# LayerNorm of an attention result: from node blocks on partitions to features on partitions

## What is computed

```python
def _layernorm(x, axis=-1, eps=1e-05):
    m = jnp.mean(x, axis=axis, keepdims=True)
    v = jnp.var(x, axis=axis, keepdims=True)
    return (x - m) / jnp.sqrt(v + eps)

# layer 0, attention over the edges, H = 4 heads of C = 32 features
ex = jnp.exp(alpha - amax[dst])
denom = jax.ops.segment_sum(ex, dst, num_segments=N)
alpha = ex / (denom[dst] + 1e-16)
msg = xj * alpha[..., None]
out = jax.ops.segment_sum(msg, dst, num_segments=N)

x = _layernorm(x + attention(x))        # the change is in this line
x = _layernorm(x + message_passing(x))  # three rounds of message passing
```

## Time and profile before

| | |
|---|---|
| Time, median of 3 runs | 10751.08 us (10739.96 to 10765.35) |
| The profiled execution, its own time | 10651.89 us |
| Span of the profiled execution | 10649.8 us |
| Busy share of the span | PE 45%, PEld 39%, DVE 47%, ACT 14%, POOL 56% |
| Mean granted TensorE clock | 0.511 of full speed |

### The profile page before, as it was taken

One profiled execution on the slowest core, in us unless ns is written; L12 is line 12 of the kernel. 1 busy time (PEld: TensorE's weight loads), 2 busy tenths in 40 slices (PEclk: granted clock), 3 DMA queues, 4 the chain that ended last, 5 costly groups with the idle time before them and its releaser, 6 DMA issues.

```text
span 10649.8 us, 148443 instructions
## 1 busy us (share of the span) xinstructions
PE 4842.9 (45%) x27078; PEld 4162.2 (39%) x27079; DVE 4985.9 (47%) x26801; ACT 1465.7 (14%) x5798; POOL 5973.7 (56%) x6332
## 2 busy tenths in 40 slices
PE   4555555555564444444445444444445444444445
PEld 3444444444453333333334333333334333333334
DVE  5545555545565444444445444444444444444445
ACT  2222222222232000000002000000002000000002
POOL 3444444444444666666663666666663666666664
PEclk6555555555555555555556555555555555555555
DMA  4333333333323333333333333333333333333333
GB/s 109 86 86 87 87 85 86 86 87 85 85 71 119 108 108 108 108 108 108 108 108 104 108 108 108 108 108 108 108 108 103 108 108 108 108 107 108 108 108 84
DMA packets 755854, 1076.13 MB, mean 101 GB/s; under 512 B 325952, under 2 KB 554464, under 8 KB 755268
## 3 DMA queue, kind: packets, MB, share of 16 engines
q0 software_dynamic: 301056, 822.48, 27.0%
q1 hardware_dynamic: 448148, 247.94, 8.7%
q10 hardware_dynamic: 6356, 3.20, 0.1%
HBM read 1027.54 MB, written 45.47 MB: 101 GB/s over the span
## 4 chain that ended last, share of the span: by engine, by line
another core or an unknown queue 45%; DVE 24%; issue 18%; PE 8%; DVEq 3%; DMA 0%; ACT 0%; SPq 0%; POOL 0%; ACTq 0%; POOLq 0%
DVE junk L1389 8%; PE ps L1588 3%; DVE ps L1368 2%; DVE pen L1378 2%; DVE acc L1409 2%; DVE selw L1398 2%; DVE junk L1026 1%; PE ps L1673 1%; PE ps L1577 1%; PE ps L1683 1%; PE ps L1585 1%; DVEq L1368 1%; PE ps L1659 1%; DVEq L988 1%
## 5 line engine op out<-in xcount | busy, mean ns | idle before, releaser
L603 POOL DMA_INDIRECT G<-mp_rows,idx x4704 | 4446.0, 945 | 2914.6 <-issue 1379.4
L1683 PE MATMUL ps<-selw,G 128*128 128x32 f32 x9408 | 2223.6, 401 | 989.2 <-issue 427.5
L1378 DVE TENSOR_TENSOR pen<-ps,G 128x512 f32<-128x512 f32 x1176 | 808.3, 687 | 3923.4 <-remote 3635.6
L1683 PEld LDWEIGHTS ps<-selw,G 128*128 128x128 f32 x9408 | 2094.2, 328 | 1272.5 <-issue 1215.9
L603 POOL DMA_INDIRECT G<-gat_rows,idx x1568 | 1487.9, 949 | 1551.2 <-ACT idx L682 1074.8
L1673 PE MATMUL ps<-awin,ring 96*128 96x128 bf16 x4704 | 717.2, 308 | 3155.0 <-DVE ring L1363 2989.1
L1673 PEld LDWEIGHTS ps<-awin,ring 96*128 96x128 bf16 x4704 | 486.6, 147 | 3260.9 <-DVE ring L1363 3081.5
L816 ACT ACTIVATE gate<-logit,cur 128x4 f32<-128x4 f32 x1176 | 349.6, 297 | 6503.1 <-issue 4053.1
L1389 DVE SCALAR_TENSOR_TENSOR junk<-pen,ps 128x128 f32<-128x128 f32 x4704 | 1061.2, 279 | 0.1
L1577 PE MATMUL ps<-sel,ex 128*4 128x32 f32 x3136 | 231.0, 238 | 1381.2 <-DVE tt L1150 1357.5
L1363 DVE TENSOR_TENSOR ring<-ring,ps 96x512 bf16<-96x512 bf16 x1176 | 796.4, 677 | 0.4
(11 more groups left out here) (182 smaller groups left out, 5409.3 us busy)
## 6 DMA issues: line engine op xcount, KB each, us to landing
ring<-rel_dst SPq DMA_DIRECT2D x1176, 96.0 KB
G<-mp_rows,idx POOLq DMA_INDIRECT x4704
ring<-rel_dst SPq DMA_DIRECT2D x392, 128.0 KB
awin<-mp_dst_rows SPq DMA_DIRECT2D x1176, 24.0 KB
G<-gat_rows,idx POOLq DMA_INDIRECT x1568
mp_rows<-acc SPq DMA_DIRECT2D x30, 640.0 KB, 3.3
mp_dst_rows<-acc SPq DMA_DIRECT2D x30, 480.0 KB
gat_rows<-ring SPq DMA_DIRECT2D x50, 128.0 KB, 2.0
```

Source lines behind the costliest of these rows:

```text
L603: pool.indirect_dma_start(out=G[:, u, width * t:width * (t + 1)], out_offset=None, in_=table, in_offset=bass.IndirectOffsetOnAxis(ap=idx[: ...
L1378: v.tensor_tensor(pen[:, off % 2, :].rearrange("p (t c) -> p t c", t=T), PS[off % 2][:, :].rearrange("p (t c) -> p t c", t=T), Grows[:, of ...
L1683: i = mm(PS[2 + off % 2][:, 0:W], Grows[:, off % U, t, 0:D], selw[:, off % 4, W * t:W * t + W], start=(t == 0), stop=(t == T - 1))
```

## The change

Nothing is turned. Chunks of 512 nodes (`LNC = 512`; `NLN = 13`, the last one 256 wide) are worked on as they lie, features on the partitions. POOL adds 1e-16 to the whole of the denominators; DVE takes the reciprocal of the whole 128x512 and multiplies; POOL adds `xT`, which is there already. The mean is taken off by a matmul with the matrix `centre` (identity minus 1/128): its product is y minus the mean over the features, on every partition. ACT squares it from PSUM, a matmul with a matrix of 1/128 gives the variance on every partition, ACT takes the root, DVE takes the reciprocal of 128x512 and multiplies into `hT`, and ACT copies `hT` to `xT`. The second load of x falls away, `weighted` is half as large, and two constants are made at the start (`centre`, `mean`) instead of one (`dsel`).

`ln_steps` writes out the order with lags, as `node_steps` does: on DVE, in one step, the second reciprocal of chunk s-3, the first reciprocal of chunk s, the scaling of chunk s-3, the product of chunk s.

```diff
+    LNC = 512
+    NLN = -(-NP // LNC)
...
+        def ln_steps(order):
+            for step in range(NLN + max(lag for lag, stage in order)):
+                for lag, stage in order:
+                    if 0 <= step - lag < NLN:
+                        stage(step - lag)
...
-            sp.wait_ge(gat["acc"], NG)
-            for b in range(NBLK):
-                load_x(b // BL, b % BL)
...
-            node_steps(pool, NT // 2, ((5, ln_residual),), BL)
+            def ln_safe_den(c):
+                nc.gpsimd.tensor_single_scalar(acc[:, 1, ln_nodes(c)], acc[:, 1, ln_nodes(c)], 1e-16,
+                                               ALU.add).then_inc(ln_safe, 1)
+            def ln_residual(c):
+                pool.wait_ge(ln_gat, c + 1)
+                nc.gpsimd.tensor_tensor(acc[:, 0, ln_nodes(c)], acc[:, 0, ln_nodes(c)], xT[:, ln_nodes(c)],
+                                        ALU.add).then_inc(ln_y, 1)
+            pool.wait_ge(gat["acc"], NG)
+            ln_steps(((1, ln_residual), (0, ln_safe_den)))
...
-            node_steps(act, NT // 2, ((0, ln_block), (7, ln_sqrt), (10, ln_to_x1), (10, ln_to_h)), BL)
+            def ln_square(c):
+                act.wait_ge(ln_yc, c + 1)
+                nc.scalar.activation(acc[:, 1, ln_nodes(c)], PS[c % 3][:, 0:ln_width(c)], ACT.Square).then_inc(ln_sq, 1)
+            def ln_sqrt(c):
+                act.wait_ge(ln_var, c + 1)
+                nc.scalar.activation(acc[:, 1, ln_nodes(c)], PS[3 + c % 3][:, 0:ln_width(c)], ACT.Sqrt,
+                                     bias=epsc[:, 0:1]).then_inc(ln_sd, 1)
+            def ln_to_x1(c):
+                act.wait_ge(ln_h, c + 1)
+                nc.scalar.copy(xT[:, ln_nodes(c)], hT[:, ln_nodes(c)]).then_inc(ln_x1, 1)
+            ln_steps(((1, ln_square), (2, ln_sqrt), (4, ln_to_x1)))
...
-            then(v.tensor_scalar(dsel[:, :], iotaF[:, 0:H], float(C), pF[:, 0:1], ALU.mult, ALU.is_equal))
+            then(v.tensor_single_scalar(centre[:, :], ident[:, :], 1.0 / D, ALU.subtract))
+            then(v.memset(mean[:, :], 1.0 / D))
...
-            node_steps(dve, NT // 2, ((8, ln_deviation), (6, ln_stats), (9, ln_scale), (2, ln_dens), (7, ln_mean_var),
-                                      (3, ln_recip), (4, ln_divide)), BL)
+            def ln_divide(c):
+                dve.wait_ge(ln_safe, c + 1)
+                v.reciprocal(acc[:, 1, ln_nodes(c)], acc[:, 1, ln_nodes(c)]).then_inc(ln_rden, 1)
+            def ln_weigh(c):
+                dve.wait_ge(ln_rden, c + 1)
+                v.tensor_tensor(acc[:, 0, ln_nodes(c)], acc[:, 0, ln_nodes(c)], acc[:, 1, ln_nodes(c)],
+                                ALU.mult).then_inc(ln_gat, 1)
+            def ln_recip(c):
+                dve.wait_ge(ln_sd, c + 1)
+                v.reciprocal(acc[:, 1, ln_nodes(c)], acc[:, 1, ln_nodes(c)]).then_inc(ln_rs, 1)
+            def ln_scale(c):
+                dve.wait_ge(ln_rs, c + 1)
+                v.tensor_tensor(hT[:, ln_nodes(c)], PS[c % 3][:, 0:ln_width(c)], acc[:, 1, ln_nodes(c)],
+                                ALU.mult).then_inc(ln_h, 1)
+            ln_steps(((3, ln_recip), (0, ln_divide), (3, ln_scale), (0, ln_weigh)))
...
-            node_steps(pe, NT // 2, ((9, ln_back), (1, ln_turn)), BL)
+            def ln_centre(c):
+                if c >= 3:
+                    pe.wait_ge(ln_h, c - 2)
+                pe.wait_ge(ln_y, c + 1)
+                mm(PS[c % 3][:, 0:ln_width(c)], centre[:, :], acc[:, 0, ln_nodes(c)], start=True, stop=True).then_inc(ln_yc, 1)
+            def ln_variance(c):
+                if c >= 3:
+                    pe.wait_ge(ln_sd, c - 2)
+                pe.wait_ge(ln_sq, c + 1)
+                mm(PS[3 + c % 3][:, 0:ln_width(c)], mean[:, :], acc[:, 1, ln_nodes(c)], start=True, stop=True).then_inc(ln_var, 1)
+            ln_steps(((2, ln_variance), (1, ln_centre)))
```

More of the change, by code:

```diff
@@ L43 @@
 PREP_IDENT = 10
-PREP_CONST = PREP_IDENT + 11
+PREP_CONST = PREP_IDENT + 12
 PREP_REL = PREP_CONST + 5
@@ L181, in gnn_kernel @@
         junk = sb("junk", [P, GE])
-        weighted = sb("weighted", [P, 4, T * D])
-        R = weighted[:, 0:2, :]
+        weighted = sb("weighted", [P, 2, T * D])
+        R = weighted[:, :, :]
         ex4 = sb("ex4", [P, 2, T * H])
@@ L244, in gnn_kernel @@
         fbcol = sb("fbcol", [P, 1])
-        dsel = sb("dsel", [P, H])
+        centre = sb("centre", [P, D])
+        mean = sb("mean", [P, D])
         WT = sb("WT", [P, D])
@@ L335, in gnn_kernel @@
         ln_y = sem("ln_y")
-        ln_st = sem("ln_st")
-        ln_mv = sem("ln_mv")
+        ln_yc = sem("ln_yc")
+        ln_sq = sem("ln_sq")
+        ln_var = sem("ln_var")
         ln_sd = sem("ln_sd")
         ln_rs = sem("ln_rs")
-        ln_rows = sem("ln_rows")
-        ln_x1T = sem("ln_x1T")
         ln_x1 = sem("ln_x1")
@@ L379, in nodes, with ln_nodes, ln_width @@
             return bass.ds(turn * (per * NB) + off * NB, NB)
+        def ln_nodes(c):
+            return slice(c * LNC, min(c * LNC + LNC, NP))
+        def ln_width(c):
+            return min(LNC, NP - c * LNC)
+        def ln_steps(order):
[3 more added lines that the diff above has]
+                        stage(step - lag)
         def spare(off):
@@ L1234, in _ @@
                 dve.sem_inc(x_free, 1)
[L1237 to L1284, removed]
-                if reached(n, off, BU):
-                    dve.wait_ge(ln_x1T, n + (off - BU + 1))
-                v.tensor_scalar(x1rows[0:NB, u, :], grows[0:NB, u, :], bmv[0:NB, u, 0:1], brs[0:NB, u, :],
-                                ALU.subtract, ALU.mult).then_inc(ln_rows, 1)
@@ new lines, in ln_recip @@
+            def ln_recip(c):
[6 more added lines that the diff above has]
+            ln_steps(((3, ln_recip), (0, ln_divide), (3, ln_scale), (0, ln_weigh)))
+            dve.wait_ge(ln_x1, NLN)
@@ L1294, in _ @@
+            dve.wait_ge(ln_h, NLN)
             dve.sem_inc(l_bn, 1)
```

33 lines of the change are left out of this document (1 added, 32 removed).

## The result

The changed kernel takes 10796.69 us (median of 8 runs, 10789.73 to 10804.40), the kernel before in the same comparison 10755.14 us (median of 8, 10739.96 to 10772.50). The ratio is 1.0038 with a 95% interval of 1.0027 to 1.0049: 41.6 us slower, and slower by more than the 0.2% that the prediction named. Predicted were 10789 us and a range of 10738 to 10828.

What follows compares the result with a forecast made beforehand. DVE was taken to bound the LayerNorm stage: full steps 100.3, start 0.8, open steps 4.3 and end 1.8 us make 107.2 against 69.6 us. That +37.6 us on the median 10751.1 gives 10788.7 us, range 10738 to 10828.

Steps and rivals of the forecast that it cites:

- The bound of the stage: LayerNorm stage, 69.6 us: DVE bounds it by seven short instructions per block; any change in its length reaches the kernel.
- R: Time of one 128x512 reciprocal on DVE, put at 3.4 us (6.5 ns per column), ends 0.61 and 5.2 us.
- POOL's addition of 1e-16: One-input addition to the denominators, once per chunk on POOL: put at 0.6 us, upper end 1.8 us.
- the loop through POOL: DVE's last instruction, POOL's residual and 1e-16, DVE's next reciprocal: 2.16 us, covered by the second reciprocal.
- the open steps 1 and 2: Early DVE steps without a second reciprocal in front, so POOL's 2.16 us are open twice: 4.3 us.
- the rival of the normal rate: DVE's reciprocal streams like other operations, R = 0.61 us: stage 57.2 us, -12.4 us, 10738.7 us; chance 0.14.
- the point from which the change loses: Reciprocal time at which the changed stage is as long as before: R = 1.6 us, with a 5.0 us step.
- Full steps: DVE steps of two reciprocals and two products, 8.02 us each, 12.5 of them: 100.3 us.
- Start: Stage start: 0.16 us of signal and 0.6 us on POOL for the first chunk, 0.8 us.
- End: Stage end: one half-width copy on ACT (0.4 us), a signal and 1.2 us of issue, 1.8 us.
- The chain over PE and ACT: From product to second reciprocal: 6.8 us per chunk, hidden behind two DVE steps of 16 us.
- From the profile to the median: The stage's +37.6 us is added to the runs' median, 10751.1 us, as the profiled execution lies 99 us under it.

Runs made afterwards that it cites:

- e8: The changed kernel, unedited, on a faster chip: 8404.35 us against 8362.66 for the kernel before, ratio 1.0050.
- e5: The kernel before without its second load of x, the block added to itself instead: ratio 1.0000 to the kernel before.
- e4: The changed kernel with POOL's residual at a lag of 2 steps in place of 1: ratio 1.0044 to the kernel before.
- e6: The changed kernel with both reciprocals as Ln and Exp on ACT, the copy on DVE, four PSUM buffers per matmul: ratio 1.0051 to the kernel before.
- e7: Edit against e6: Abs_reciprocal_sqrt, squared for the denominator, replaces Ln and Exp on ACT: 8334.26 us, ratio 0.9966 to the kernel before.
- e9: The changed kernel with chunks of 256 nodes in place of 512: ratio 1.0060 to the kernel before.
- e1: The changed kernel with both DVE reciprocals replaced by products of the same shape, result not normalised: ratio 1.0005 to the kernel before.
- e0: The kernel before, unedited, profiled a second time: span 10754.6 us, stage 69.6 us.
- e3: Edit against e1: POOL's residual at a lag of 2 steps in place of 1: ratio 0.9995 to the kernel before.

## Why the prediction was right

**The bound of the stage, and that its length is paid in full.** Right. The stage is 37.4 us longer, the kernel 41.6 us (29 to 53 by the interval), and e8 gives 41.7 at another total. e5 shows that the removed load was hidden, as the prediction said. The 4 us between are within the interval, but they come back. On the two fast chips, where the runs of a kernel lie closer together, the medians of e4, e6, e7, e8 and e9 are 3.3, 2.6, 3.7, 4.3 and 7.0 us above what their stages explain, and that of e5, which has the old layout, 0.4. So something of 3 to 4 us outside the stage seems to belong to the changed kernel; no run shows what. It isn't a later rise of PE's clock, for which the prediction had thought of 0 to 2 us: over the 33.4 us behind the stage the granted clock is 0.91 in both kernels.

**The reciprocal's rate.** This decided the case. Predicted 6.5 ns per column and R = 3.4 us, measured 6.3 ns and 3.26 us from start to start (3.21 for the first reciprocal). The value came from comparing equal shapes, the 4-column reciprocal and the 4-column addition. That was the soundest comparison at hand, but it rests on 22 ns between two short instructions, and other readings of such rows gave 4.0, 4.7, 8.5 and 10 ns. That it came so close owes something to luck. The Trainium skill, "VectorE: DVE Perf Modes", walkthrough of the 8-slice pipeline, names a repeat count of 8, from which the prediction made an estimate of 8.4 ns. No run agrees with that as a rate per column: the measured ratio to a product's 1.05 ns is 6.

**POOL's addition of 1e-16.** Wrong: 0.6 us predicted, 1.49 measured, slower than the two-input residual (1.26, predicted 1.4). I had placed it near a memset because it has one input. So the loop through POOL takes 2.95 us and not 2.16, and the second reciprocal is only 0.3 us longer than what it covers. The forecast survived, since R stayed above; the open steps 1 and 2 cost 5.9 us instead of 4.3. But the rival of the normal rate was priced wrongly by this. It was to end at -12.4 us; e1, which stands in for it, has a stage 2.7 us longer than before. Some of that is e1's own: its products make POOL's residual longer in nine steps, 3.6 us in all, which a reciprocal, with one input, need not do. Without them the stage would be about 69 us, by this estimate. So the point from which the change loses lay near R = 0.6 us and not at 1.6. (The residual's 1.4 us were taken from an intercept of 119 ns, called POOL's shortest instruction; four memsets of one column in the same trace take 98 to 118 ns. That moves the 1.4 us by less than 0.1.)

**The terms of the sum.** The stage was computed as 107.2 us and measured as 107.0. The terms are less exact than that. Full steps: 12.5 x 7.62 = 95.2 us against 100.3, because R was 0.14 us too long and the products overlap more (0.54 and 0.60 us from start to start). Start: 2.9 us against 0.8; POOL needs 1.5 us, and 1.3 us more pass before DVE's first reciprocal, which the profile puts down to issue and no run explains. The kernel before has 2.9 us at the same place too, but there they are put down to PE. Open steps: 5.9 against 4.3. End: 1.7 against 1.8. Together 105.7, and the other 1.3 us lie in the steps at both ends, above all in products that wait for the reciprocal just before them (3.39 us from start to start, instead of 3.2). Errors of -5.1 and of +5.0 us cancel.

**The chain over PE and ACT.** Hidden, as predicted: DVE never waits for ACT in the changed kernel. Square and the root shared a table, only one load stands in the stage. But there was less to spare than the 16 us against 6.8 of the prediction. By the lags, ACT makes the root of a chunk only behind the square of the next one:

```profile
3209.40 0.60 ACT L747 ACTIVATE acc<-ps 128x512 f32<-128x512 f32 x1 [5.93 <-PE ps L1569]
3209.89 0.68 ACT L751 ACTIVATE acc<-ps,epsc 128x512 f32<-128x512 f32 x1
```

This root ends at 3210.57, and DVE's reciprocal of it starts at 3213.35, so 2.8 us are left. For the first chunk, whose root has the table load in front, it is 0.8 us (3189.67 to 3190.51). In e4 the first chunk's variance is ready at 2111.87, but its root starts only at 2115.53, behind the next chunk's square and the table load: that is the 2.63 us of waiting.

**From the profile to the median.** Adding the stage's difference to the median of the runs, and not to the profiled execution, was right: e0 shows that the profile of before lay about 105 us under a second one of the same kernel.

## What to carry to other kernels

Before work moves from one value per node to a full tile, count the columns of every operation whose price per column is above a product's. Here the reciprocals went from 5 columns per 128 nodes to 256, and at six times the price of a product they cost more than fewer and longer instructions gave. The way out was on another engine, with a function that shares its table with its neighbours. And an engine in a loop with another is covered only by what stands in its queue in front of the wait: speed that instruction up, and the loop appears.

## What the runs showed of the hardware

- A reciprocal on DVE takes 3.35 us for 128x512 f32 and 1.74 us for 128x256, 6.3 ns per column, against 1.05 ns for a product.
- POOL's one-input addition (1.49 us for 512 columns, 0.85 for 256) is slower than its two-input one (1.26 and 0.72).
- DVE's products with both inputs in SBUF and instructions of POOL can slow each other: DVE's product from 0.69 to as much as 1.75 us, POOL's residual from 1.26 to 1.64 and 1.79 us and its 1e-16 from 1.49 to 1.81 us (e1, e3). Beside a reciprocal of DVE, POOL keeps its 1.26 us, and beside POOL a product with one input in PSUM keeps its 0.68 us.
- `Ln` and `Exp` in turn cost a table load of 1.28 us each time (e6); `Abs_reciprocal_sqrt` and `Square` in turn don't, and take 0.48 to 0.75 us from start to start for 512 columns (e7).
- The same program takes 10.76 and 10.78 ms in two comparisons and 8.36 ms on two other chips. The difference lies outside this stage, which takes 107.0 us on both; 1070 us of it lie in front, nearly all in the attention's edge loop (the stage begins at 3169.6 and at 2099.8 us).
